# CIN recommender tower on one core: the low halves of a group's split products, from GpSimd to VectorE

## The reference, cut to what matters

```
z   = einsum('bfd,bgd->bfgd', x0, xk).reshape(b, f * g, d)   # all products
cur = einsum('bpd,pm->bmd', z, W)                            # W: f0, f1, f2
outs.append(cur);  xk = cur                                  # three times
z   = sum over d of concatenate(outs, axis=1)                # 1024 x 384
h   = relu([z, dense_ctx] @ W_top1 + b_top1)
h   = relu(h @ W_top2 + b_top2);  y = h @ W_top3
```

## Time and profile before

| | before |
|---|---|
| median of 3 executions | 1338.92 us (1338.18 to 1340.23) |
| span of the profiled execution, from its first to its last instruction | 1331.2 us |
| whole time of the profiled execution | not listed |
| TensorE matmul / weight load busy | 1271.8 / 951.9 us (96% / 72%) |
| VectorE busy | 973.0 us (73%) |
| ScalarE busy | 733.6 us (55%) |
| GpSimd busy | 1046.5 us (79%) |
| 93 low halves on GpSimd (L246) | 118.5 us, 1290 ns each |
| TensorE's granted clock | 0.999 of full speed over the span |

### The profile page before, as it was taken

The page is one execution under the profiler, slowest core; times in us unless marked ns, Lnnn a source line. Parts: engine busy times, 40 slices in busy tenths (PEclk is TensorE's granted clock), DMA queues, the critical chain, the costliest instruction groups (busy, mean ns, idle before and its releaser), DMA issues.

```text
span 1331.2 us, 25256 instructions
## 1 busy us (share of the span) xinstructions
PE 1271.8 (96%) x5493; PEld 951.9 (72%) x5493; DVE 973.0 (73%) x3253; ACT 733.6 (55%) x2422; POOL 1046.5 (79%) x937
## 2 busy tenths in 40 slices
PE   0799999999999999999999999999999999999999
PEld 0477777777787777777777776877777777877765
DVE  4677786888758787777868887578876778688740
ACT  4365564656546565555646565456655566466641
POOL 6568888788878898688887988779887888876540
PEclk9999999999999999999999999999999999999999
DMA  7632221222211222122212222122222221221000
GB/s 169 172 89 66 67 58 33 61 55 65 63 46 47 61 66 60 54 65 66 52 37 59 56 65 63 29 59 66 60 60 59 66 57 41 55 56 55 2 1 1
DMA packets 121771, 78.48 MB, mean 59 GB/s; under 512 B 77437, under 2 KB 89827, under 8 KB 121653
## 3 DMA queue, kind: packets, MB, share of 16 engines
q1 hardware_dynamic: 106124, 73.45, 19.7%
q0 software_dynamic: 10240, 2.64, 2.6%
q10 hardware_dynamic: 5288, 1.32, 0.5%
HBM read 18.50 MB, written 2.63 MB: 16 GB/s over the span
## 4 chain that ended last, share of the span: by engine, by line
PE 66%; DVE 15%; issue 8%; POOL 4%; ACT 2%; DMA 2%; SPq 1%; DVEq 1%; ACTq 0%; POOLq 0%
PE ps L516 15%; PE ps L520 14%; PE ps L517 14%; PE ps L495 13%; DVE terms L835 11%; PE ps L540 5%; DVE prods L807 3%; PE ps L530 3%; POOL terms L433 3%; PE ps L599 2%; ACT terms L686 2%; PE ps L609 1%; POOL x_in L405 1%; DMA dense_rows<-in_dense_ctx 1%; DMA w<-in_f 1%
## 5 line engine op out<-in xcount | busy, mean ns | idle before, releaser
L835 DVE SCALAR_TENSOR_TENSOR terms<-ps,x_scal,terms 128x128 f32<-128x128 f32 x2944 | 807.0, 347 | 280.9 <-ACT terms L686 171.4
L686 ACT ACTIVATE terms<-ps,x_scal 128x128 f32<-128x128 f32 x2048 | 584.0, 376 | 412.1 <-PE ps L520 267.3
L433 POOL TENSOR_TENSOR terms<-terms 128x1024 f32<-128x1024 f32 (+2 forms) x384 | 566.1, 1474 | 106.0 <-DVE terms L835 85.0
L516 PE MATMUL ps<-w_high,x_high 128*128 128x512 f32 (+1 forms) x1280 | 590.0, 461 | 25.0 <-DVE terms L835 16.8
L520 PE MATMUL ps<-w_high,x_low 128*128 128x512 f32 (+1 forms) x1280 | 497.3, 389 | 0.0
L517 PE MATMUL ps<-w_low,x_high 128*128 128x512 f32 (+1 forms) x1280 | 495.8, 387 | 0.0
L405 POOL DMA_INDIRECT x_in<-in_tables,row_at x320 | 303.7, 949 | 89.8 <-issue 69.8
L516 PEld LDWEIGHTS ps<-w_high,x_high 128*128 128x128 f32 x1280 | 240.6, 188 | 154.3 <-DVE terms L835 65.2
L517 PEld LDWEIGHTS ps<-w_low,x_high 128*128 128x128 f32 x1280 | 241.6, 189 | 67.0 <-issue 28.1
L520 PEld LDWEIGHTS ps<-w_high,x_low 128*128 128x128 f32 x1280 | 240.3, 188 | 49.5
L495 PE MATMUL ps<-prods,w 117*128 117x512 f32 x262 | 135.1, 601 | 9.2 <-DVE prods L807 9.2
(11 more groups left out here) (48 smaller groups left out, 416.2 us busy)
## 6 DMA issues: line engine op xcount, KB each, us to landing
prods<-x_cols SPq DMA_DIRECT2D x190, 234.0 KB
x_cols<-x_rows SPq DMA_DIRECT2D x93, 78.0 KB
x_first<-x_cols SPq DMA_DIRECT2D x93, 78.0 KB
x_in<-in_tables,row_at POOLq DMA_INDIRECT x320, 2.4
x_diag<-x_scal SPq DMA_DIRECT2D x256, 9.8 KB
s<-in_f SPq DMA_DIRECT2D x3, 832.0 KB, 11.5
x_rows<-x_in SPq DMA_DIRECT2D x31, 80.0 KB, 2.4
wt<-in_W_top SPq DMA_DIRECT2D x1, 768.0 KB, 13.1
```

What stands on the lines that cost most here:

```text
L433: nc.gpsimd.tensor_tensor(t[:, 0:n], t[:, 0:n], t[:, n:2 * n], ALU.add).then_inc(s_tree, 1)
L516: nc.tensor.matmul(y, x1_high[:, par, at:at + P], high, start=True, stop=False)
L686: op = nc.scalar.activation(terms[:, u % 2, FB * ACT_BANKS.index(q) + i, :], ps[:, (BANKS * u + q) % RING, i * G:(i + 1) * G], ACT.Copy, s ...
L835: nc.vector.scalar_tensor_tensor(out=acc, in0=y, scalar=x0, in1=acc, op0=ALU.mult, op1=ALU.add).then_inc(s_mac, 1)
```

## The change

GpSimd no longer makes the low halves. VectorE makes them, in tile 1 behind its banks 4, 5 and 6 (bank 5 is ScalarE's, so low halves 0 and 1 follow each other). The semaphore gets another name, and TensorE waits for it in the same place. Nothing else is moved.

```diff
-POOL_LOWS = {0: (0, 1), 1: (2,)}
+LOWS = ((1, 4), (1, 5), (1, 6))
...
-        def split_low(eng, gf, i):
-
-            eng.wait_ge(s_high, (gf - 1) * NS + i + 1)
-            eng.tensor_tensor(prods_low[:, i, :], prods[0:KR, SPLIT[i], :],
-                              prods_high[:, i, :].bitcast(F32), ALU.subtract).then_inc(low_ready(gf, i)[0], 1)
...
-            def add_up(bt, u, front=True):
+            def add_up(bt, u):
 
-                gf = bt * GROUPS + u // TILES + 1
-                if front:
-                    for i in POOL_LOWS.get(u % TILES, ()):
-                        split_low(pool, gf, i)
                 t = terms[:, u % 2]
...
                     i = SPLIT.index(k)
-                    pe.wait_ge(*low_ready(gf, i))
+                    pe.wait_ge(s_low, gf * NS - NS + i + 1)
...
+            def split_low(gf, i):
+
+                dve.wait_ge(s_high, gf * NS - NS + i + 1)
+                nc.vector.tensor_tensor(prods_low[:, i, :], prods[0:KR, SPLIT[i], :],
+                                        prods_high[:, i, :].bitcast(F32), ALU.subtract).then_inc(s_low, 1)
...
                         multiply(bt, j, PRODUCTS.index((tile, q)), X1_BANK)
+                    if front and (tile, q) in LOWS:
+                        split_low(gf, LOWS.index((tile, q)))
```

More of the change, by code:

```diff
@@ L200, in cin_tower @@
         s_high = sem("product_highs_ready")
-        s_plow = sem("product_lows_by_pool")
+        s_low = sem("product_lows_ready")
         s_x1 = sem("x1_summed")
@@ L235, in cin_tower @@
         CREDIT_A, CREDIT_MAC, CREDIT_X2, CREDIT_S3, CREDIT_S3E, CREDIT_R = NA, MACS, 2, 2, 1, 1
-        POOL_PARTS = [i for parts in POOL_LOWS.values() for i in parts]
-        def low_ready(gf, i):
-            return s_plow, (gf - 1) * len(POOL_PARTS) + POOL_PARTS.index(i) + 1
-        def split_low(eng, gf, i):
-            eng.wait_ge(s_high, (gf - 1) * NS + i + 1)
-            eng.tensor_tensor(prods_low[:, i, :], prods[0:KR, SPLIT[i], :],
-                              prods_high[:, i, :].bitcast(F32), ALU.subtract).then_inc(low_ready(gf, i)[0], 1)
         def banks_before(kind, n):
@@ L459, in _ @@
                     pool.wait_ge(s_put, (NBATCH * GROUPS - 2) * 16)
-                add_up(NBATCH - 1, u, u < STEPS - TILES)
+                add_up(NBATCH - 1, u)
                 if u < TILES:
```

## The result

| | before | after |
|---|---|---|
| median of 4 executions | 1339.09 us | 1345.38 us (1342.67 to 1346.89) |
| ratio to before | | 1.0047, 95% interval 1.0035 to 1.0059 |
| span of the profiled execution | 1331.2 us | 1343.4 us (its whole time: 1345.2) |
| VectorE busy | 973.0 us | 1044.6 us |
| GpSimd busy | 1046.5 us | 962.2 us |

The change makes the kernel slower by 6.3 us, 0.47%. The forecast was 1351, the range 1336 to 1358. 1345.4 stands just inside the lower edge of what the prediction gave to contention (1345 to 1358) and 2 us above what it gave to a free port (1338 to 1343), so the time alone would not have told the two apart; the stretches do.

A forecast was written before the change was run, and what follows sets the result against it. TensorE, busy 96% of the span, was taken to bound the kernel. The terms -17.6 + 19.6 + 6.7 + 3.7 gave +12.4 us on the median of 1338.92, forecast 1351 us, range 1336 to 1358.

The forecast's parts named there:

- contention: VectorE's subtractions, both sources in SBUF, wait for GpSimd's running adds; the forecast's own case, 1345 to 1358 us, chance 0.58.
- a free port: VectorE's subtractions take 0.68 us everywhere, never waiting for GpSimd's adds; rival, 1338 to 1343 us, chance 0.24.
- Relief: With the low halves off GpSimd, every four-tile stretch starts on time: a gain of 17.6 us.
- TensorE's wait for low half 0: First split matmul of tile 1: TensorE waits the whole subtraction, 0.85 us in 23 stretches, +19.6 us.
- Contention in B: Second four-tile stretch of seven batches: low half 0 waits 0.95 us for GpSimd's 512-wide add, +6.7 us.
- Ties in C and D: Third and fourth stretches, and the last second one: subtraction and GpSimd's last add arrive together, 0.23 us each, +3.7 us.
- I take half: Where subtraction and GpSimd's last add arrive together, half of that add's 0.46 us, 0.23, is charged as wait.
- no contention: Subtractions take 0.68 us everywhere, so TensorE's new wait and GpSimd's relief cancel: 1341 us, chance 0.24.
- relief alone: VectorE's train starts sooner and hides TensorE's new wait: 1321 us, in part 1322 to 1336; chance 0.12.
- a second wait: Tile 2: VectorE, held by GpSimd, gives bank (1, 6) too late for (2, 1): 13.8 us more, 1365 us, chance 0.06.

The follow-up runs named there:

- the late sum: Changed kernel plus one spare 768-column GpSimd add ahead of tile 0's sum in the third and fourth stretches of seven batches: 1357.97 us, x 1.0149.
- all three edits: Changed kernel with unsplit factor first, subtractions behind banks (1, 6), (1, 8), (1, 9), and renumbering between GpSimd's third and last add: 1325.57 us, x 0.9897.

## Why the prediction was right

The sign and the mechanism held; the loss was half of what was forecast (6.3 us for 12.4). By its terms:

- **Relief, -17.6.** Measured -20.3, in the run without low halves, with the first product at T+3.20 in every stretch but the first. What was missing is the A of 47.3 us in the earlier trace rows's kernel, 1.9 us late by a pause of GpSimd. I had the stretch in the trace and left it out of the sum as an accident of one execution. It stands in both profiles of the kernel before, and the pause in all twelve profiles.
- **TensorE's wait for low half 0, 23 x 0.85 = +19.6.** Measured +19.6, from the run with the renumbering later less the one without low halves. Its parts are right too: in C the subtraction takes 0.69, the first split matmul starts 0.75 late, and (2, 0) 0.85 late (T+17.46 for T+16.61 without low halves). The wait is in B, C and D and not in A, as said; the first A has one of 0.67 us, where the forecast took a wait for a weight load to cover it, and no run isolates that one.
- **Contention in B, 7 x 0.95 = +6.7.** Measured +7.9. The direct wait was 0.91 (the first split matmul at T+17.04 in B against T+16.13), and there was a second one of 0.16 at (2, 1), which my working had allowed in the range only. The two make 1.07 of the 1.17 us that B loses to contention; the rest I did not trace.
- **Ties in C and D, +3.7.** Measured 0. The step that failed is "I take half": low half 0 took 0.68 to 0.70 us in all fourteen C and D and in the last B and C, so it was no coin, and GpSimd's add paid, 1.5 to 1.6 us for 0.46, which TensorE does not feel. By the prediction's own numbers GpSimd's last add, 4.75 us behind the end of (0, 9), came 0.09 ahead of low half 0, 4.84 behind it, which would have meant a wait of 0.37; they leave out the 0.08 us until GpSimd starts on its sum. In the trace the add starts 0.02 us behind the subtraction in C and 0.1 behind it in D. In the last B and C it starts up to 0.02 ahead and still loses. The one exception, the first D, where the add starts 0.31 behind low half 0 and gets in ahead of low half 1 (0.94 us), costs 0.04 us.

The sum by these is -20.3 + 19.6 + 7.9 = +7.2 us for the stretches. That it meets the measured +7.2 is no further proof, since each term is the difference of two of the same four profiles. The forecast of +12.4 is too high by the ties (3.7), the pause (1.9) and tenths of the relief (0.8), and too low by 1.2 of contention.

The choice of contention over a free port rested on one row of 1157 ns, a thin ground, and it came out right: the source in PSUM takes the wait away, and the late sum makes it elsewhere. The row itself stands up to a second look. In the first profile of the kernel before, it meets a gather of GpSimd (first two lines), and in the second profile of the same kernel it takes 1.09 us and the gather takes 1.56 for 0.94 (last two):

```profile
18.84 1.16 DVE L853 TENSOR_TENSOR w<-terms 117x896 f32<-117x896 f32 x1
18.87 0.94 POOL L405 DMA_INDIRECT x_in<-in_tables,row_at  x1 [0.30 <-issue]
...
17.23 1.09 DVE L853 TENSOR_TENSOR w<-terms 117x896 f32<-117x896 f32 x1
17.58 1.56 POOL L405 DMA_INDIRECT x_in<-in_tables,row_at  x1 [0.30 <-issue]
```

In eight of the twelve profiles a gather that starts while this instruction runs takes 1.3 to 1.9 us; in three others the instruction takes 1.12 to 1.16. The Trainium skill ("SBUF — State Buffer", Who interferes with whom) gives the same rule, and the trace agrees: 2.74 us for a pair against 1.27 with one source in PSUM. Of "whichever issues first" the records show that the recorded start alone doesn't tell it when the lead is under 0.1 us.

The rival "no contention" would have B at 36.9, which is what the source in PSUM and the later renumbering give; it was wrong for this kernel by GpSimd's moment in B only. The rival "relief alone" asked for a VectorE train that starts sooner than T+3.2; it never does, not even without low halves. The rival "a second wait" exists in B with 0.16 us, and is 0.3 per stretch once the first wait is gone (the unsplit factor first).

## What to carry to other kernels

Work moved from a late engine to an early one pays only if the place where its result is wanted moves too: here the relief was worth 20 us, a wait of exactly one subtraction, 23 times, took it all back, and contention in B made it a loss; wanting the unsplit factor first and putting the subtractions behind their neighbours' urgent banks gave most of it back (x 0.989). A VectorE instruction with both sources in SBUF must be placed against GpSimd's time line as well as VectorE's own. And a late stretch in one profile may be a fixed event of the program: look for it in a second one before leaving it out.

## What the runs showed that I had not expected

- A pause of 2.19 us of GpSimd between two gathers in the sixth batch, in all twelve profiles (at 815, 819, 822 and 802 us in the first four), always ahead of the 224th of the 320 gathers. A like one of 2.2 us stands ahead of the 114th (at 386 us in the kernel before) and lengthens no stretch. So it goes by the count of gathers and not by the time; what makes it is not shown. It costs 1.9 us when GpSimd is late and nothing when it isn't.
- When VectorE is first, GpSimd's 128-wide add waits for both subtractions of the pair, 1.59 us, not only for the first.
- In the run with the unsplit factor first, the B in which GpSimd came 0.15 us later than in the others lost 1.5 us less: a small delay of GpSimd handed the wait from VectorE to it.
- A gather of GpSimd waits for the subtraction too, if it starts while one runs or just ahead of it; one that starts 0.26 us or more ahead takes its 0.95. With one source in PSUM no gather of the loop takes longer than 0.97. In B with all three edits, GpSimd and then VectorE:

```profile
571.31 1.58 POOL L393 DMA_INDIRECT x_in<-in_tables,row_at  x1 [0.21 <-issue]
...
571.38 0.68 DVE L797 TENSOR_TENSOR prods_low<-prods,prods_high 117x512 fp32r<-117x512 f32 x1
```
